# State-space stage of a decoder layer: y summed by accumulating transposes, B rows spread by the tensor engine

## The reference

```python
xz = x @ W_in;  xb, z = split(xz)
xb = silu(causal_conv4(xb) + conv_b)
dt_low, Bm, Cm = split(xb @ W_x, [64, 80])
dt = softplus(dt_low @ W_dt + b_dt)
h = h * exp(A * dt_t) + (x_t * dt_t) * B_t       # per channel and state, over t
y = sum_n h * C_t
out = ((y + xb * D) * silu(z)) @ W_out
```

## Time and profile before

| what | before |
|---|---|
| median of 3 runs | 1614.55 us (1614.25 to 1616.75) |
| profiled execution, first to last instruction | 1611.6 us |
| state-space stage | up to 914 us, its first scan at 39 us |
| busy of the span: PE, DVE, ACT, POOL | 89%, 79%, 68%, 78% |
| mean granted TensorE clock | 0.946 of 2.4 GHz |

### The profile page before, as it was taken

The page is one execution under the profiler, slowest core; times in us unless marked ns, Lnnn a source line. Parts: engine busy times, 40 slices in busy tenths (PEclk is TensorE's granted clock), DMA queues, the critical chain, the costliest instruction groups (busy, mean ns, idle before and its releaser), DMA issues. The chain is left out here.

```text
span 1611.6 us, 22055 instructions
## 1 busy us (share of the span) xinstructions
PE 1430.3 (89%) x6146; PEld 876.3 (54%) x6146; DVE 1269.8 (79%) x2207; ACT 1088.3 (68%) x2118; POOL 1250.6 (78%) x861
## 2 busy tenths in 40 slices
PE   4889999899989989998998799999999999539994
PEld 1334343334333433343343388888888877429993
DVE  1999999999999999999999367777777787624542
ACT  4778877887788778877886477666666655114552
POOL 1899999999999999999999444477777766624665
PEclk8999999999999999999999889999999999659997
DMA  5455465546554655465545263314418000036771
GB/s 167 154 178 182 153 198 168 184 153 205 168 184 153 196 176 176 161 197 176 169 161 159 63 220 130 136 35 142 149 47 327 14 8 13 22 112 189 210 208 38
DMA packets 126058, 236.92 MB, mean 147 GB/s; under 512 B 13490, under 2 KB 76917, under 8 KB 125952
## 3 DMA queue, kind: packets, MB, share of 16 engines
q1 hardware_dynamic: 121408, 227.21, 43.6%
q0 software_dynamic: 4544, 8.47, 1.5%
HBM read 180.89 MB, written 55.66 MB: 147 GB/s over the span
## 5 line engine op out<-in xcount | busy, mean ns | idle before, releaser
L388 POOL TENSOR_TENSOR hc<-state,c_rows 128x1024 f32<-128x1024 f32 x256 | 598.5, 2359 | 46.4 <-DVE state L585 40.7
L585 DVE TENSOR_TENSOR_SCAN state<-ps_da,inp 128x512 f32<-128x512 f32 x512 | 593.4, 1206 | 27.3 <-ACT ps_da L481 27.3
L704 PE MATMUL ps_y<-hc,ident 128*128 128x512 f32 x1024 | 491.0, 619 | 56.2 <-POOL hc L388 56.2
L481 ACT ACTIVATE ps_da<-dt,a_neg 128x512 f32<-128x512 f32 x512 | 345.4, 688 | 86.8 <-DVE state L585 84.2
L704 PEld LDWEIGHTS ps_y<-hc,ident 128*128 128x128 f32 x1024 | 194.2, 196 | 296.4 <-issue 208.6
L574 DVE TENSOR_TENSOR inp<-dtx,ps_b 128x1024 f32<-128x1024 f32 x192 | 230.8, 1202 | 37.6 <-POOL dtx L359 22.6
L1069 POOL TENSOR_TENSOR rs<-ms,m_half 128x4 f32<-128x4 f32 x48 | 67.9, 1415 | 124.0 <-DVE ms L1267 123.8
L1192 ACT ACTIVATE ex<-sc,nmx,ctx_r 77x128 f32<-77x128 f32 x192 | 92.4, 482 | 97.3 <-DVE nmx L1280 97.3
L371 POOL TENSOR_TENSOR inp<-dtx,b_rows 128x1024 f32<-128x1024 f32 x64 | 151.0, 2359 | 0.1
L627 PE MATMUL ps_misc<-x1T,w_conv 128*128 128x512 f32 (+3 forms) x256 | 118.2, 606 | 23.1 <-ACT x1T L414 23.1
L487 ACT COPY ps_b<-b_rows 128x512 f32<-128x512 f32 x192 | 111.1, 579 | 37.8 <-DVE inp L574 36.3
(11 more groups left out here) (234 smaller groups left out, 2689.6 us busy)
## 6 DMA issues: line engine op xcount, KB each, us to landing
b_rows<-bc_rows SPq DMA_DIRECT2D x128, 512.0 KB, 4.7
c_rows<-bc_rows SPq DMA_DIRECT2D x128, 512.0 KB, 4.0
sorted_x<-pad_rows SPq DMA_DIRECT2D x8, 4160.0 KB
w<-in_L_ffn_W SPq DMA_DIRECT2D x78, 256.0 KB
vw<-vw_rows SPq DMA_DIRECT2D x16, 462.0 KB
vw_rows<-vw_out SPq DMA_DIRECT2D x16, 384.0 KB
xrow<-sorted_x SPq DMA_DIRECT2D x39, 130.0 KB
x_tok<-in_x SPq DMA_DIRECT2D x16, 256.0 KB, 4.1
```

The source lines that it names most:

```text
L388: pool.tensor_tensor(hc[:, n % RING], state[:, n % RING], over_c(c_rows[:, slot, n % 2]), ALU.mult).then_inc(hc_ready, 1)
L481: act.activation(ps_da[u % DA_RING][:], dt[:, par, c], ACT.Exp, scale=a_neg[:, c, n:n + 1]).then_inc(da_ready, 1)
L585: dve.tensor_tensor_scan(state[:, n % RING, c], ps_da[u % DA_RING][:], inp[:, n % RING, c], 0.0, ALU.mult, ALU.add).then_inc(state_ready, 1)
L704: ins = pe.matmul(ps_y[:, c], ident[:], hc[:, n % RING, c], start=False, stop=n == NS - 1)
```

## The change

y is kept token-major: `ps_y` is [tokens, sequence, half, channels], each state is added by eight transposes of 128 columns that accumulate in PSUM (`is_transpose`), the D term by eight f32 products, and z is computed token-major too. After the gating y is turned back by eight transposes and two ScalarE copies (`turn_y`, `turned`). B is turned once a group (`BT`, four transposes and a copy), and for each of DVE's twelve feeds TensorE spreads one column of it over the partitions into `ps_b` by four transposes (`spread_b`); ScalarE's copy `copy_b` is gone, and DMA brings only GpSimd's four B rows. xb of the next group and z share one visit to the silu table in slot 4. `add_y` runs two slots behind; `POOL_FEEDS` and the slot tables change; the gating moves from slot 2 to 3, the normalising from 15 to 12. The number of DVE's and GpSimd's large operations stays.

```diff
-    POOL_FEEDS = [3, 7, 11, 15]
+    POOL_FEEDS = [1, 6, 9, 13]
-    PE_UNIT = {5: "P", 9: "K", 13: "V0", 14: "V1", 15: "V2"}
-    ACT_UNIT = {6: "P", 10: "K", 14: "V0", 15: "V1"}
+    PE_UNIT = {9: "P", 10: "K", 11: "V0", 12: "V1", 13: "V2"}
+    ACT_UNIT = {10: "P", 11: "K", 12: "V0", 13: "V1", 14: "V2"}
-    PE_SLOT = {0: ["xT"], 1: ["xb0"], 2: ["xb1"], 5: ["dbl"], 7: ["dt0", "dt1"]}
-    ACT_SLOT = {1: ["xT"], 4: ["xb0", "xb1"], 6: ["dbl"], 8: ["relu0", "abs0", "relu1", "abs1"], 9: ["exp", "ln"]}
+    PE_SLOT = {0: ["xb0"], 1: ["xb1"], 5: ["dbl"], 6: ["BT"], 7: ["dt0", "dt1"]}
+    ACT_SLOT = {0: ["xT"], 5: ["dbl"], 6: ["BT"], 8: ["relu0", "abs0", "relu1", "abs1"], 9: ["exp", "ln"]}
...
@@ ScalarE, group
+                for c in range(C):
+                    if n < NS - 1:
+                        decay(g, par, n + 1, c)
+                    elif not last:
+                        decay(g + 1, 1 - par, 0, c)
+                if n == 4:
+                    act.preload_act_table_set("silu_and_others")
+                    if not last:
+                        prepare(g + 1, 1 - par, "xb0")
+                        prepare(g + 1, 1 - par, "xb1")
+                    gates(g)
+                    act.preload_act_table_set("natural_log_exp_and_others")
+                if not first and n == 5:
+                    turned(g - 1, 0)
+                if not first and n == 6:
+                    turned(g - 1, 1)
...
@@ TensorE
+        def fill_z(g, k, last):
+            if not last:
+                pe.wait_ge(act_pre, apre(f"xb{k}", g + 1))
...
+            for b in range(2):
+                at = (g * GB + 2 * k + b) * P
+                ins = pe.matmul(ps_misc[BANK[f"z{k}"]][:, b * C * P:(b + 1) * C * P], x1T[:, at:at + P], w_in[:, C * P:], start=True, stop=True)
+            ins.then_inc(z_full, 1)
+        def start_y(g, par):
+            need(pe, yz_ready, g)
+            for b in range(GB):
+                for c in range(C):
+                    pe.matmul(ps_y[:, b, c], xb[:, par, c, b * P:(b + 1) * P], d_diag[:, c], start=b % 2 == 0 and c == 0, stop=False, skip_group_check=True)
         def add_y(g, par, n):
+            pe.wait_ge(hc_ready, after(NS, n, g))
+            for b in range(GB):
+                for c in range(C):
+                    ins = pe.matmul(ps_y[:, b, c], hc[:, n % RING, c, b * P:(b + 1) * P], ident[:], start=False, stop=n == NS - 1,
+                                    is_transpose=True, skip_group_check=True)
+            ins.then_inc(y_added, 1)
+        def spread_b(g, par, n):
...
+            need(pe, dve_fed, fed_count(DVE_FEEDS, g, n) - 1)
+            for b in range(GB):
+                ins = pe.transpose(ps_b[:, b * P:(b + 1) * P], b_tok[:, par, b, n:n + 1].broadcast_to([P, P]), ident[:])
+            ins.then_inc(b_spread, 1)
...
         def group(g, par, first, last):
             for n in range(NS):
+                if n + 2 in DVE_FEEDS:
+                    spread_b(g, par, n + 2)
+                elif n + 2 == NS and not last:
+                    spread_b(g + 1, 1 - par, 0)
+                if n == 4:
+                    fill_z(g, 0, last)
+                    fill_z(g, 1, last)
+                if n < 2 and not first:
+                    add_y(g - 1, 1 - par, NS - 2 + n)
+                if n == 4:
+                    start_y(g, par)
+                    add_y(g, par, 0)
+                    add_y(g, par, 1)
+                if n == 5:
+                    add_y(g, par, 2)
+                if n >= 5:
+                    add_y(g, par, n - 2)
+                if not first and n in (5, 6):
+                    turn_y(g - 1, n - 5, last)
                 if not last:
                     for name in PE_SLOT.get(n, []):
                         fill_misc(g + 1, 1 - par, name)
...
+                if n == NS - 1 and g + 2 < NG:
+                    fill_misc(g + 2, par, "xT")
```

More of the change, by code:

```diff
@@ L379, in group @@
                 slot = n // 2 % SLOTS
[L380 to L383, removed]
+                pool.wait_ge(state_ready, after(U, n * C + C - 1, g))
+                need(pool, y_added, after(NS, n, g) - RING)
+                pool.wait_ge(c_loaded[slot], c_value(g, n))
                 if first and n == 1:
@@ L441, in gates, with turned @@
         def gates(g):
-            act.preload_act_table_set("silu_and_others")
             need(act, yz_ready, g)
[L444 to L447, removed]
+            for k in range(2):
+                act.wait_ge(z_full, after(2, k, g))
+                act.activation(sz[:, 2 * k:2 * k + 2].rearrange("p b f -> p (b f)"), ps_misc[BANK[f"z{k}"]][:], ACT.Silu).then_inc(z_gated, 1)
+        def turned(g, c):
+            act.wait_ge(yt_full, after(C, c, g))
+            if c == 0:
+                need(act, tail_full, after(2, 0, g - 1))
+            act.copy(yzT[:, c], ps_misc[BANK[f"y{c}"]][:]).then_inc(yt_read, 1)
         def centred(g):
@@ L476, in decay @@
         def decay(g, par, n, c):
-            u = n * C + c
-            if u == 0:
+            if n == 0 and c == 0:
                 act.wait_ge(pool_pre, ppre("first", g))
[L480 to L486, removed]
-            act.copy(ps_b[:], b_rows[:, slot, n % 2]).then_inc(b_copied, 1)
-        for n in range(NS):
-            for name in ACT_SLOT.get(n, []):
-                prepare(0, 0, name)
-        copy_b(0, 0)
+            need(act, state_ready, op_free(g, n, c))
+            act.activation(op_bank(g, n, c)[:], dt[:, par, c], ACT.Exp, scale=a_neg[:, c, n:n + 1]).then_inc(da_ready, 1)
+        prepare(0, 0, "xT")
+        act.preload_act_table_set("silu_and_others")
+        prepare(0, 0, "xb0")
+        prepare(0, 0, "xb1")
+        act.preload_act_table_set("natural_log_exp_and_others")
+        for name in ("dbl", "BT", "relu0", "abs0", "relu1", "abs1", "exp", "ln"):
+            prepare(0, 0, name)
         act.wait_ge(s_loaded, 16 * 7)
@@ L596, in group @@
                 scan(g, par, n, 1)
[L597 removed]
+                if not first and n == 3:
                     gated(g - 1)
[L599 removed]
+                if not first and n == 12:
                     normed(g - 1)
[L601 removed]
+        over_groups(group)
         gated(NG - 1)
@@ new lines, in turn_y @@
+        def turn_y(g, c, last):
+            if c == 0:
+                pe.wait_ge(yz_ready, g + 1)
+                if g < NG - 1:
+                    pe.wait_ge(z_gated, after(2, 0, g + 1))
+                else:
+                    pe.wait_ge(u_read, unit("V2", g))
+            else:
+                pe.wait_ge(yt_read, after(C, 0, g))
+            for b in range(GB):
+                ins = pe.transpose(ps_misc[BANK[f"y{c}"]][:, b * P:(b + 1) * P], yz[:, b, c], ident[:])
+            ins.then_inc(yt_full, 1)
@@ L714, in _ @@
+        fill_misc(0, 0, "xT")
+        pe.wait_ge(w_loaded, 16 * NW)
+        pe.wait_ge(w_scaled, KW)
+        for name in ("xb0", "xb1", "dbl", "BT", "dt0", "dt1"):
+            fill_misc(0, 0, name)
         pe.wait_ge(w_scaled, KW + 7)
@@ L730, in group @@
                 if not first and n == 9:
-                    project(g - 1, last)
-                if n == 11:
-                    fill_z(g, 0, last)
-                    fill_z(g, 1, last)
-                if not first and n == 13:
+                    project(g - 1)
+                if not first and n == 10:
                     variance(g - 1)
```

277 lines of the change are left out of this document (125 added, 152 removed).

## The result

The changed kernel takes 1778.34 us (median of 4 runs, 1774.38 to 1779.37) against 1614.78 for the kernel before beside it: 1.1006 times as long, 95% interval 1.0991 to 1.1022. The prediction was 1780, slower at 0.90.

A forecast was written before the change was run, and what follows sets the result against it. DVE was taken to be in front, 51.4 us of work in a 53.94 us period. Nine chain steps summed to 65.3; 14.5 x (65.3 - 53.94) = 165, plus 1 at the end, gave 1780 us, own range 1730 to 1890.

The forecast's parts named there:

- b: TensorE's state 14, xb0, spread 3 and hand-over: 4.81 us at full clock, 6.71 with 3.7 us at half rate.
- both places: TensorE's slots 0 to 2 and slot 4, where B-row spreads queue behind long work: 14.5 x (65.3 - 53.94) = 165 us.
- Rival 1: TensorE's clock stays full despite the gaps: period 61.7 us, time 1728; chance 0.20.
- rival 2: TensorE at half rate throughout, its parts of the chain doubled: period 81.2 us, time 2010; chance 0.04.
- Rival 3: Only the second place costs, as GpSimd lags less at state 14: 56.5 to 58.3 us, time 1654 to 1681; chance 0.09.
- second place: TensorE's slot 4: spread 7 queues behind z, D term and two states, while DVE has only 3.4 us to do.
- Rival 4: Faster: spread 7 in time, xb0 ahead of spread 3, GpSimd's 51.4 to 51.6 us sets the period: 1580; chance 0.07.
- e to g: Slot 4, ScalarE's decay, table, xb0, then TensorE's z to spread 7: 8.5 us by the rows, 3.4 needed to be faster.
- Rival 5: Waits only change places, nothing measurable comes of it: period within 0.2 of 53.94 us; chance 0.03.

The follow-up runs named there:

- experiment 2: Changed kernel with TensorE making xb0 and xb1 of the next group in slots 2 and 3 instead of 0 and 1: 1725.06 us, 1.0677.
- experiment 1: Changed kernel with the accumulating transposes of y replaced by f32 products with the identity: 1875.46 us, 1.1607.
- experiment 8: Kernel before, with ScalarE's copies of B rows left out and DVE's feeds reading the rows from SBUF: 1755.54 us, 1.0863.
- experiment 5: Changed kernel with the D term's 16 products issued two more times ahead of z, to keep TensorE busy: 1782.51 us, 1.1033.

## Why the prediction was right

The steps, measured in one group from feed 8 (459.24) to the next feed 8 (524.64), all from timelines (468.22 is the start of DVE's feed behind that scan):

| step | predicted, us | measured, us |
|---|---|---|
| i) DVE to the end of state 9's scan, 468.22 | 8.97 | 8.98 |
| a) GpSimd's ten operations, to 492.00 | 23.65 | 23.78 |
| b) state 14, xb0, spread 3, to 498.56 | 6.71 | 6.56 |
| c) state 15, xb1, spread 4, to 503.27 | 4.71 | 4.71 |
| d) DVE, to decay 510.15 | 6.70 | 6.88 |
| e) decay, table, xb0, to 512.89 | 2.62 | 2.74 |
| f) z, to 516.13 | 3.6 | 3.24 |
| g) D term, states, spread 7, to 520.30 | 4.0 | 4.17 |
| h) states, turn, dbl, spread 8, to 524.64 | 4.36 | 4.34 |
| sum | 65.3 | 65.40 |

What was off:
- b holds in every other group only. In the others the granted clock was full at xb0 (3.56 us at 558.31) and feeds 2 and 3 waited 0.92 and 2.41 us in place of 5.05. So the mean period is 64.50, not 65.3: 0.8 x 14 = 11 us too many. Where it holds it came out a little short of 6.71: the 3.7 us at half rate taken from the earlier trace rows were read some 0.3 us long, since the windows at either end of that stretch, 413 to 414 and 416 to 417, stand at 0.65 and 0.64.
- Group 0 has both places and group 1 the first of them before the first gating; I counted half a place. The first gating came at 117.51, 15.9 us later than 101.57, where 5.7 were forecast: 10 too few. The end, from the fifteenth gating on, took 752.2 us, 2.6 less, where +1 was forecast. 15.9 + 14 x 10.55 - 2.6 = 161.0, the span's growth. These errors nearly cancelled, so the closeness of 1780 is in part luck.
- These figures are of the profiled run, the shortest of the four (1774.38). The others took 4 to 5 us more at a mean granted clock of 0.893 in place of 0.898; without a trace of them it is not known how many of their groups had xb0 at half rate.
- An accumulating transpose cost the 0.11 us taken from the plain one.
- Rival 1 (full clock) failed at z in every group and at xb0 in every other one; rival 2, because xb1, z's followers and dbl ran at full clock (3.56, 1.91, 1.88). Rival 3 failed by the 6.3 us ahead of feeds 3 and 4; experiment 2, which has the second place alone, took 1725, above its 1654 to 1681, as feed 7 then waits 7.94. Rival 4 was to be decided at e to g: they took 10.15 us, not 3.4. Rival 5 failed with the period.

On the rule of the Trainium skill named in the prediction ("TensorE: Matmul & The Clock Gate", Part 4), that transposes don't raise the engine to its full clock, the rows don't agree. Transposes with gaps did sit at 0.50 where products sat at 1.00 (experiment 1). But the changed kernel has what the trace before lacked, a stretch of transposes alone, 485.05 to 489.85 (the eight at 488.81 and 489.25 are transposes too), and in it the clock came back:

```profile
485.05 1.97 PE L731 MATMUL ps_y<-ident,hc 128*128 128x128 f32 x8 [1.97 <-POOL hc L399]
487.37 1.61 PE L731 MATMUL ps_y<-ident,hc 128*128 128x128 f32 x8 [0.35 <-POOL hc L399]
```

```profile
486.00:488.00 2.00, 1.65 (x8) 1.25 (x7) 2.00 (x3) 0.73 (x2) 2.00 (x2) 0.50 0.00 0
488.00:490.00 2.00, 1.85 (x15) 1.61 (x13) 2.00 (x2) 1.58 (x3) 2.00 (x2) 0.88 0.81 205
```

The sixteen transposes at 517.91, between products, ran at full clock as well (1.91 us). Why products kept the clock at 1.00 ahead of xb0 in experiment 1 stays open.

## What to carry to other kernels

Moving an operand's making from an engine with slack to TensorE adds little work and puts each consumer behind everything queued ahead of it; so read the queue slot by slot, and ask of each short producer which wait stands before it. When one stall is mended, look for the next thing behind the same wait: spread 7 moved alone won nothing, while moving xb0 and xb1 behind two spreads and z behind the sums as well won 138 us. The cheap gain was in the kernel before all along: half of one of the two waits in its profile, 6.4 of the 12.6 us ahead of feeds, went when two ScalarE operations no longer shared a slot.

## What the runs showed of the hardware that I had not expected

DVE and GpSimd hold each other up when DVE's operand moves from PSUM to SBUF: a GpSimd product went from 2360 to 3055 ns in the mean, and single feeds to 3365 (experiment 8). ScalarE's copies into PSUM, which look like waste, buy 0.7 us on a GpSimd product in the mean. I had it as a rival only. The Trainium skill has it: "SBUF — State Buffer", in "SBUF: two separate sides", says that GpSimd and a DVE operation with two SBUF inputs lock each other out for a whole instruction; feeds at either 1197 or up to 3365 agree. And the granted clock was at 0.58 in the mean of 506 to 508 in experiment 5, where TensorE had stood since 505.80, while in the changed kernel, where it had stood since 505.20, the same window was still at 1.00. So the length of the gap alone doesn't tell the two apart; what does stays open.
